# Softmax attention with two heads on the two halves of TensorE's rows, and a causal mask made as a product

## What is computed

```python
s = q[b, h] @ k[b, h].T / sqrt(8)        # 1024 x 1024
s = s + slope[h] * (key - query)         # layer 1 only
s = where(key <= query, s, -inf)         # causal
p = softmax(s, axis=-1)
y = p @ v[b, h]
```

## Time and profile before

| | |
|---|---|
| median of 3 runs | 2875.7 us (2871.59 to 2876.74) |
| span of the profiled execution | 2867.6 us |
| time of the profiled execution itself | not given beside its span |
| PE busy | 2232.3 us (78%) |
| DVE busy | 1650.8 us (58%) |
| ACT busy | 1246.7 us (43%) |
| POOL busy | 727.9 us (25%) |
| mean granted TensorE clock | 0.870 |

### The profile page before, as it was taken

One profiled execution on the slowest core, in us unless ns is written; L12 is line 12 of the kernel. 1 busy time (PEld: TensorE's weight loads), 2 busy tenths in 40 slices (PEclk: granted clock), 3 DMA queues, 4 the chain that ended last, 5 costly groups with the idle time before them and its releaser, 6 DMA issues. The chain is left out here.

```text
span 2867.6 us, 44223 instructions
## 1 busy us (share of the span) xinstructions
PE 2232.3 (78%) x15437; PEld 1302.5 (45%) x15454; DVE 1650.8 (58%) x3303; ACT 1246.7 (43%) x1901; POOL 727.9 (25%) x870
## 2 busy tenths in 40 slices
PE   3778878863899989999740389999999788777474
PEld 2555555542344444444340134444443686455274
DVE  6676767631677747567049277777775343553201
ACT  2343434320466656565520046565666343332143
POOL 1435353441010101000000223233322113663432
PEclk8898888876899999999755599999999899896597
DMA  2111100012011101110000302121210895110185
GB/s 62 39 53 53 46 2 2 2 44 85 2 55 40 54 24 32 46 36 20 1 1 3 106 22 77 42 79 40 79 54 27 257 321 185 41 41 22 38 274 182
DMA packets 144303, 185.77 MB, mean 65 GB/s; under 512 B 26970, under 2 KB 118267, under 8 KB 138976
## 3 DMA queue, kind: packets, MB, share of 16 engines
q1 hardware_dynamic: 103295, 137.52, 16.0%
q0 software_dynamic: 13696, 32.02, 3.5%
q10 hardware_dynamic: 27126, 13.75, 1.7%
HBM read 130.46 MB, written 52.21 MB: 64 GB/s over the span
## 5 line engine op out<-in xcount | busy, mean ns | idle before, releaser
L1743 DVE TENSOR_REDUCE a_mpart<-a_mx 128x1 f32<-128x512 f32 (+3 forms) x1216 | 741.2, 655 | 284.4 <-PE a_mx L1497 148.8
L1653 ACT ACTIVATE a_prob<-a_st 128x1024 f32<-128x1024 f32 (+3 forms) x768 | 607.1, 812 | 487.8 <-PE a_st L1533 374.4
L1497 PE MATMUL a_mx<-a_ka,a_qa 96*128 96x512 bf16 (+3 forms) x1536 | 428.8, 339 | 31.6 <-DVE a_mpart L1743 14.4
L1530 PE MATMUL a_st<-a_qa,a_ka 96*128 96x512 bf16 (+3 forms) x1536 | 416.3, 333 | 29.9 <-ACT a_prob L1653 22.8
L1548 PE MATMUL a_acc<-a_prob,a_v_aug 128*9 128x512 f32 (+3 forms) x3072 | 321.1, 494 | 0.0
L1497 PEld LDWEIGHTS a_mx<-a_ka,a_qa 96*128 96x128 bf16 x1536 | 140.7, 99 | 315.6 <-DVE a_mpart L1743 175.4
L1426 POOL DMA_INDIRECT x_rows<-l_xn,l_slots x128 | 125.4, 980 | 400.0 <-ACT a_prob L1653 390.0
L1533 PE MATMUL a_st<-w_mask_t,identb 128*128 128x128 bf16 x1024 | 208.8, 224 | 0.0
L1530 PEld LDWEIGHTS a_st<-a_qa,a_ka 96*128 96x128 bf16 x1536 | 145.7, 99 | 136.5 <-ACT a_prob L1653 38.6
L2084 PE MATMUL t_psu<-t_xsT,t_w 128*128 128x128 f32 x960 | 152.8, 294 | 23.9 <-DMA t_w<-in_l_experts 17.4
L1500 PE MATMUL a_mx<-w_mask_q,identb 128*128 128x128 bf16 x768 | 165.2, 225 | 0.0
(11 more groups left out here) (438 smaller groups left out, 4055.0 us busy)
## 6 DMA issues: line engine op xcount, KB each, us to landing
t_w<-in_l_experts SPq DMA_DIRECT2D x160, 192.0 KB, 4.2
t_w<-in_l_experts SPq DMA_DIRECT2D x40, 514.0 KB, 7.4
a_qa<-q_parts_dram SPq DMA_DIRECT2D x96, 192.0 KB
a_ka<-k_parts_dram SPq DMA_DIRECT2D x96, 192.0 KB
x_rows<-zeros SPq DMA_DIRECT2D x25, 512.0 KB, 3.6
t_xs<-x_rows ACTq DMA_DIRECT2D x40, 256.0 KB, 4.9
y_rows<-t_y POOLq DMA_DIRECT2D x40, 256.0 KB, 5.1
q_parts_dram<-a_parts SPq DMA_DIRECT2D x24, 256.0 KB, 3.0
```

The costliest lines, as they stand in the source:

```text
L1497: ins = pe.matmul(to, qa[G % NQ][:, h0 + k, qi * P:(qi + 1) * P], ka[G % NQ][:, h0 + k, lo:hi], start=not masked_first, stop=k == per - 1 ...
L1530: ins = pe.matmul(to[:, lo:HALF], ka[G % NQ][:, h, j * P:(j + 1) * P], qa[G % NQ][:, h, ch * HALF + lo:(ch + 1) * HALF], start=True, stop= ...
L1653: act.activation(prob[:, v % NP_, 2 * pair:2 * pair + 2, lo:HALF], sring[s % 2][:, :, lo:HALF], ACT.Exp, scale=1.0 if alibi else scale).th ...
L1743: dve.tensor_reduce(mpart[:, G % 2, h0:h0 + per, qi, piece], slot[:, 0:per * width].rearrange("p (k w) -> p k w", k=per), X, ALU.max).then ...
```

## The change

Six of the nine pairs of parts are kept (`TERMS`), 48 rows; with bias and maxima a head has 54 rows (51 in layer 2). A pair of heads lies on two halves of the partitions, rows from 0 and rows from 64, so `qa` and `ka` hold 128 rows x 2 head pairs x 1024 tokens. The parts are stored to DRAM in the order of the terms, so six copies of each operand instead of three, and loaded with four DMAs. The mask is the product of two factors of 64 rows, `tri_row` and `tri_col`, of which each half of the partitions has a copy; they are made once, in layer 0 (`tri_cut` and `tri`). A max event covers heads of one side; the two sides of an event stand next to each other in `order`.

```diff
+TERMS = ((0, 0), (0, 1), (0, 2), (1, 0), (1, 1), (2, 0))
+DOT_ROWS = len(TERMS) * DH
+TILE = 64
+BAR = -2.0 ** 46
+FADE = 2.0 ** -80
...
-    common = weights(ctx, [(name, [P, P]) for name in ("mask_t", "mask_q", "earlier")], BF16)
+    common = weights(ctx, [("earlier", [P, P])], BF16)
+    tri_row = sb(ctx, "tri_row", [P, P], BF16)
+    tri_col = sb(ctx, "tri_col", [P, P], BF16)
...
+                        elif kind == "tri":
+                            pe.wait_ge(tri_s, 1)
+                            for side in range(2):
+                                for copy in range(2):
+                                    ins = pe.matmul(slot[copy * TILE:(copy + 1) * TILE, side, 0:P], identb[:, 0:P:2], tri_b[:, side],
+                                                    start=True, stop=True)
...
+                        elif kind == "tri_cut":
+                            up = tri_f[:, 0]
+                            link(dve.tensor_copy(up, W["earlier"][:]))
+                            link(dve.tensor_tensor(up[:, 1:], up[:, 1:], ident[:, 0:P - 1], ALU.subtract))
+                            link(dve.tensor_scalar(up, up, BAR / FADE, None, ALU.mult))
+                            dve.scalar_tensor_tensor(tri_b[:, 0, 1:], ident[:, 0:P - 1], BAR, up[:, 1:], ALU.mult, ALU.add)
+                            dve.tensor_copy(tri_b[:, 0, 0:1], up[:, 0:1])
+                            dve.scalar_tensor_tensor(tri_b[:, 1, 1:], ident[:, 0:P - 1], FADE, ident[:, 1:], ALU.mult, ALU.add)
+                            dve.tensor_copy(tri_b[:, 1, 0:1], ident[:, 0:1]).then_inc(tri_s, 1)
+                        elif kind == "tri":
+                            dve.tensor_copy(tri_row[:], slot_of(e)[:, 0, 0:P])
+                            dve.tensor_copy(tri_col[:], slot_of(e)[:, 1, 0:P]).then_inc(ring_v, 1)
...
-        max_rows = QK_ROWS + (PARTS if alibi else 0)
+        max_rows = DOT_ROWS + (PARTS if alibi else 0)
...
-                    per = min(GH, HALF // width)
-                    out += [("max", G, qi, piece, h, per) for h in range(0, GH, per)]
+                    per = min(GH // 2, HALF // width)
+                    out += [("max", G, qi, piece, side, k, per) for k in range(0, GH // 2, per) for side in range(2)]
...
+                    if goal and ahead[goal - 1][0] == "max" and ahead[goal - 1][4] == 0:
+                        goal += 1
...
-            qa = [sb(c, f"{n}qa{i}", [QK_PAD, GH, T], BF16) for i in range(NQ)]
-            ka = [sb(c, f"{n}ka{i}", [QK_PAD, GH, T], BF16) for i in range(NQ)]
+            qa = [sb(c, f"{n}qa{i}", [P, GH // 2, T], BF16) for i in range(NQ)]
+            ka = [sb(c, f"{n}ka{i}", [P, GH // 2, T], BF16) for i in range(NQ)]
...
-                                for s in range(PARTS):
-                                    sp.dma_start(dram[b % 2, s].rearrange("e h t -> h e t"), parts[i][:, s]).then_inc(qk_stored, 16)
+                                for s, term in enumerate(TERMS):
+                                    sp.dma_start(dram[b % 2, s].rearrange("e h t -> h e t"), parts[i][:, term[i]]).then_inc(qk_stored, 16)
...
-                            for p1 in range(PARTS):
-                                r = slice(p1 * PARTS * DH, (p1 + 1) * PARTS * DH)
-                                sp.dma_start(qa[i][r], q_parts_dram[b % 2, p1:p1 + 1, :, hs].to_broadcast([PARTS, DH, GH, T])
-                                             ).then_inc(qk_loaded[i], 16)
-                                sp.dma_start(ka[i][r], k_parts_dram[b % 2, :, :, hs]).then_inc(qk_loaded[i], 16)
-                            if alibi:
-                                sp.dma_start(ka[i][QK_ROWS:max_rows], a["alibi"][:, hs]).then_inc(qk_loaded[i], 16)
-                            sp.dma_start(qa[i][max_rows:rows], a["zero_rows"][0:PARTS]).then_inc(qk_loaded[i], 16)
+                            sp.wait_ge(qk_stored, n_store * 16 * (b + 1))
+                            for side in range(2):
+                                hs = slice(G % NG * GH + side, (G % NG + 1) * GH, 2)
+                                for to, dram in ((qa[i], q_parts_dram), (ka[i], k_parts_dram)):
+                                    sp.dma_start(to[rows_of(side, 0, DOT_ROWS)], dram[b % 2, :, :, hs]).then_inc(qk_loaded[i], 16)
+                                if alibi:
+                                    sp.dma_start(ka[i][rows_of(side, DOT_ROWS, max_rows)], a["alibi"][:, hs]).then_inc(qk_loaded[i], 16)
...
-                            sp.dma_start(qa[G % NQ][max_rows:rows, :, ch * HALF:(ch + 1) * HALF],
-                                         m_parts_dram[u % 2].rearrange("(s h q) t -> s h (q t)", s=PARTS, h=GH)).then_inc(m_loaded[u % 2], 16)
+                            back = m_parts_dram[u % 2].rearrange("(s k e q) t -> e s k (q t)", s=PARTS, k=GH // 2, e=2)
+                            for side in range(2):
+                                sp.dma_start(qa[G % NQ][rows_of(side, max_rows, rows), :, ch * HALF:(ch + 1) * HALF], back[side]
+                                             ).then_inc(m_loaded[u % 2], 16)
...
+                            r, half = rows_of(side, 0, max_rows), rows_of(side, 0, TILE)
                             last_piece = piece == qi // 4
-                            diagonal = W["mask_q"][:]
-                            if width == P and last_piece:
-                                pe.matmul(slot[:].rearrange("p (k w) -> p k w", k=per), identb[:],
-                                          diagonal.unsqueeze(1).to_broadcast([P, per, P]), start=True, stop=False)
                             for k in range(per):
                                 to = slot[:, k * width:(k + 1) * width]
-                                masked_first = width == P and last_piece
-                                ins = pe.matmul(to, qa[G % NQ][:, h0 + k, qi * P:(qi + 1) * P], ka[G % NQ][:, h0 + k, lo:hi],
-                                                start=not masked_first, stop=k == per - 1 if masked_first else not last_piece)
-                                if last_piece and not masked_first:
-                                    ins = pe.matmul(to[:, width - P:width], identb[:], diagonal, start=False, stop=True)
+                                ins = pe.matmul(to, qa[G % NQ][r, k0 + k, qi * P:(qi + 1) * P], ka[G % NQ][r, k0 + k, lo:hi],
+                                                start=k == 0, stop=not last_piece, skip_group_check=True)
+                                if last_piece:
+                                    ins = pe.matmul(to[:, width - P:width], tri_col[half], tri_row[half], start=False, stop=True,
+                                                    skip_group_check=True)
...
-                            for k in range(2):
-                                h = 2 * pair + k
-                                to = sring[s % 2][:, k]
-                                ins = pe.matmul(to[:, lo:HALF], ka[G % NQ][:, h, j * P:(j + 1) * P],
-                                                qa[G % NQ][:, h, ch * HALF + lo:(ch + 1) * HALF], start=True, stop=not diag)
-                                if diag:
-                                    ins = pe.matmul(to[:, lo:lo + P], identb[:], W["mask_t"][:], start=False, stop=True)
+                            for side in range(2):
+                                r = rows_of(side, 0, rows)
+                                ins = pe.matmul(sring[s % 2][:, side, lo:HALF], ka[G % NQ][r, pair, j * P:(j + 1) * P],
+                                                qa[G % NQ][r, pair, ch * HALF + lo:(ch + 1) * HALF], start=True, stop=not diag)
+                            if diag:
+                                for side in range(2):
+                                    half = rows_of(side, 0, TILE)
+                                    ins = pe.matmul(sring[s % 2][:, side, lo:lo + P], tri_row[half], tri_col[half], start=False, stop=True)
...
-                            dve.tensor_reduce(mpart[:, G % 2, h0:h0 + per, qi, piece],
-                                              slot[:, 0:per * width].rearrange("p (k w) -> p k w", k=per), X, ALU.max).then_inc(ring_v, 1)
+                            here = mpart[:, G % 2].rearrange("p (k e) q i -> p e k q i", e=2)[:, side, k0:k0 + per, qi, piece]
+                            dve.tensor_reduce(here, slot[:, 0:per * width].rearrange("p (k w) -> p k w", k=per), X, ALU.max).then_inc(ring_v, 1)
```

50 lines of the change are left out of this document (29 added, 21 removed).

## The result

| | before | after |
|---|---|---|
| median | 2875.0 us (2871.59 to 2876.74, 4 executions) | 2805.5 us (2795.1 to 2810.98, 4 executions) |
| ratio after : before | | 0.9751 (95%: 0.9731 to 0.9771) |
| span of the profiled execution | 2867.6 us | 2802.9 us |
| PE, DVE, ACT busy | 2232.3, 1650.8, 1246.7 us | 2125.4, 1648.8, 1248.1 us |
| mean granted TensorE clock | 0.870 | 0.843 |

The change is 70 us faster (2.5%). I had forecast 146 us less and a range that ended at 2800: the sign was right, the size was not. The profiled execution itself took 2804.6 us, 1.7 more than its span; so of the 8.1 us that I added between span and median most was the scatter of one execution.

The account below looks back on a forecast made before the run. PE's streaming was taken to bound each group: -3.6-2.1+0.6+0.7 = -4.4 us, over 28 groups -123; first and last groups -6, layer starts -20, Mamba +2, and 8.1 from span to median gave 2729 us, range 2660 to 2800.

Parts of the forecast that it names:

- Halves overlap: Score and max products of a quiet group: two heads' row halves run side by side, -3.6 and -2.1 us a group.
- DVE and ring waits, +0.7: Quiet group: PE comes near DVE's 26.6 us and waits on the ring of three PSUM slots, +0.7 us a group.
- Shape changes, +0.6: PE in a quiet group: eight more changes of product shape at 0.09 us each, +0.6 us a group.
- Groups with side work keep it whole: their f32 products stay.: Softmax-layer groups with side work: they get the full gain of a quiet group, -4.4 us each.
- Queues at the layers' start, -10 each: DMA at each layer's start: doubled stores +7 us, smaller loads save more, -10 us a layer, bounds +7 and -20.
- The added 7 us lie in that: Later in a layer: the doubled stores' added 7 us fit in some 17 steps before the parts are used.
- Mamba layer, +2: Making `tri_cut` and `tri`: nine DVE operations and four matmuls add 2 us, bounds 0 and 5.
- the fourth: Rival on PE's clock: it falls to 1.2 GHz through all groups, each near 55 us, total over 3400; chance 0.02.
- rival 1: The ring keeps max pairs apart, only scores gain: -2.3 us a group, quiet group 30.4, total 2788 us; chance 0.15.
- Rival 3: Row halves take turns at a price per change: total 2943 us at 0.02 us, 3140 at 0.09; chance 0.11.
- Any group longer than 32.7: Sign of being wrong: any group taking longer than 32.7 us, the time of one quiet group before the change.
- the alarm at 0.9: Sign of being wrong: a granted clock below 0.9 in the stretch of the 14 groups.

## Why the prediction was wrong

By its own steps, against the profiled spans:

- **Halves overlap.** Right. A masked step took 0.28 us (0.30), and PE alone gained 5.2 us a group (5.1). The split into scores and maxima has no meaning of its own: in the run with halved reductions the scores' overlap was worth 1.6 us, not 3.6.
- **DVE and ring waits, +0.7.** Mis-sized: 1.9. A quiet group gained 3.3 us instead of 4.4. I added VectorE's busy time to 0.5 us of gaps and called 26.6 a floor far enough away. But 25.9 us of PE and 25.8 us of VectorE over three slots gave 29.4; here two engines of equal length that take turns on three slots took 3.5 us more than either alone. Over 28 groups this is 1.2 x 28 = 34 us of the shortfall.
- **Shape changes, +0.6.** Not measured by itself. In the 64-row run of the kernel before, the step from a product to the f32 transposes takes 0.32 us (893.77 to 894.09) for 0.23 with 96 rows (877.04 to 877.27), which fits the 0.09; the step behind the maxima's bf16 transpose takes 0.17 with either, so not every border costs it.
- **"Groups with side work keep it whole: their f32 products stay."** This is the step that failed. They lost 20 us in layer 1 instead of gaining 31. I had even written that shorter products and ring waits lower the clock, and then gave it a price only in the extreme case in which all groups run at 1.2 GHz, with a chance of 0.02. The middle case had no term: a clock of 0.98 that becomes 0.91 (0.90 in the change's second profile). At 1.2 GHz a quiet group with all products on one half took 58.28 us for 32.62, 1.8 times as long; by that some 35 of the added 102 - 23 = 79 us are lost, an estimate. In layer 2 the clock fell from 1.00 to 0.97, which is the rest: 31.7 gained where 14 light groups of 3.2 would give 45.
- **Queues at the layers' start, -10 each.** The mechanism held, and the size was at my bound: from the first store to the end of the first group 20.2 us in layer 1, and 11.4 up to the same place in layer 2, first groups included. I had weighed slow 2 KB pieces against it; they didn't show.
- **"The added 7 us lie in that"** (a store later in the layer). Wrong: I looked for who uses the parts, not for what else stands in SP's queue behind the twelve stores. `a_even` did, VectorE waited 2.9 us for it, and PE behind VectorE 3.8. Moving the two transfers made that group 4.7 us shorter.
- **Mamba layer, +2.** The profiled execution was 10.2 us later at layer 1's first store. But three profiles of the kernel before (one with 64 rows, one with halved reductions) reached the layer's first transfer at 632.0 to 640.5 us and seventeen of the changed code's family at 634.5 to 642.9: +2 lies well within that scatter.
- **The rivals.** None of the four was the case as it stood; the fourth named the mechanism, and priced only its extreme. The quiet group, 29.4, lies between forecast (28.3) and rival 1 (30.4). Rival 3's second figure is a slip: its own terms at 0.09 us give 120 x 0.09 + 0.7 = 11.5 us a group and 3178 us, not 3140; nothing else uses it. My signs of being wrong were badly set. "Any group longer than 32.7" was true of groups with side work before the change (41.0 to 56.4 us); read as "longer than before" it came, in five groups of layer 1. The clock of 0.91 in layer 1's stretch stayed just above the alarm at 0.9, though 0.07 of clock over 567 us was worth eight groups' forecast gain (35 us). Scores that wait for `m_parts` in mid-layer didn't come.

Shares of the 82 us between the span forecast and measured: what is left for the clock, and for the waits that came with it, once the ring is taken off, 43 in layer 1 and 13 in layer 2; the ring 34, Mamba 8; against them the starts 9 and the tail 7. The last three are of one execution each.

What is shown: rows in use change how the clock behaves (two pairs of runs that differ in nothing else on PE, though their transfers or exponentials differ), and in the changed kernel waits of 1.8 us let it fall (filled, it falls half as often). What is only argued: that in the changed kernel itself the longer stretches, up to 13.7 us, come from the half-array products and not from the waits that grew in number; no run has the overlap with all rows in use, since there is none. That the clock falls behind eight waits of eight instead of three of eight speaks for the products. Not every fall has a wait ahead of it: three of the seven stretches at 1.2 GHz before and four of the seventeen after begin with no wait of over 0.6 us in the 8 us ahead. All seven begin within or up to 2 us behind a set of the gated network's one-row f32 products; that these let the clock fall is not tested by itself.

## To carry to other kernels

When a change makes PE's work shorter or narrower in a stretch where it waits now and then, put a term for the granted clock beside the gain: take each group's clock from the windows, and for each 0.01 that it could fall nearly 1% of the stretch (here 0.07 and 35 of 567 us). Look at groups with side work apart, and ask of each added transfer what stands behind it in its queue. Where a known wait lets the clock fall, overwritten products in a PSUM bank that is free anyway can bring more than they cost: 21 us in 14 groups of one layer here, of which 10 to 13 reached the total.

## What the runs showed that I had not expected

- PE busy for 100% of 124 us at 1.2 GHz without the clock rising, with scores, maxima and masks on 51 to 64 of 128 rows; the same instructions on all rows ran at 2.4 GHz.
- The scatter of one kernel follows the clock. Six executions of the change, span and mean granted clock: 2790.3 at 0.850, 2792.8 at 0.847, 2802.7 at 0.843, 2807.2 at 0.841, 2810.0 at 0.840, 2811.4 at 0.838. Where in the side work a stretch at 1.2 GHz begins differs between executions.
- Products of different kinds, with different operands and PSUM banks, overlap as well as a pair does when they lie on different halves of the rows and stand side by side in the program.
